# Attention unrolled, its small steps moved, and its transposing transfers cut in two

## The reference

```
qkv = (x @ Wqkv).reshape(b, l, 3, H, DH)          # 16 heads of 16 features
q = q * cos + rotate_half(q) * sin                # the same for k
scores = einsum("bqhd,bkhd->bhqk", q, k) * 16 ** -0.5
out = einsum("bhqk,bkhd->bqhd", softmax(scores), v).reshape(b, l, d) @ Wo
x = layernorm(x + out)
x = layernorm(x + ffn(x))      # a shared expert, and the top 2 of 8 experts per token
```

## Time and profile before

| | |
|---|---|
| median of 3 runs | 1282.6 us (1282.54 to 1285.19) |
| the profiled execution | 1286.31 us |
| its span, first to last instruction | 1284.4 us |
| mean granted TensorE clock | 0.969 |
| TensorE busy | 1174.9 us, 91% of the span |
| VectorE, ScalarE, GpSimd busy | 970.9, 895.0, 582.5 us |
| DMA | 194.45 MB, 260558 packets, 152256 of them under 512 B |
| transposing transfers (`att_qk<-att_stack`) | 128 |

### The profile page before, as it was taken

How to read it: one execution, slowest core, us unless ns; L and a number is a source line. 1 busy time by engine, 2 the same in 40 slices (tenths; PEclk the granted TensorE clock), 3 DMA queues, 4 the chain that set the end, 5 groups by cost and what they waited for, 6 DMA issues and landing times. The chain is left out here.

```text
span 1284.4 us, 27380 instructions
## 1 busy us (share of the span) xinstructions
PE 1174.9 (91%) x8369; PEld 864.1 (67%) x8416; DVE 970.9 (76%) x1868; ACT 895.0 (70%) x1970; POOL 582.5 (45%) x591
## 2 busy tenths in 40 slices
PE   3799898989898999879899969999999999999997
PEld 2333333333333333247899969999999999999897
DVE  4788787888787888738766658777777777777596
ACT  3377777777677777647744447777777777777686
POOL 5332222232223220006557745666666666666763
PEclk8699999999999999989899979999999999999999
DMA  6743525252537363532032256777777777776363
GB/s 151 137 82 58 112 53 97 63 110 61 130 96 159 85 155 88 170 125 85 17 112 92 96 170 220 258 237 235 249 251 252 237 238 234 249 252 207 131 187 114
DMA packets 260558, 194.45 MB, mean 151 GB/s; under 512 B 152256, under 2 KB 243392, under 8 KB 260480
## 3 DMA queue, kind: packets, MB, share of 16 engines
q1 hardware_dynamic: 253664, 174.82, 48.2%
q0 software_dynamic: 6816, 18.75, 4.1%
HBM read 122.06 MB, written 37.52 MB: 124 GB/s over the span
## 5 line engine op out<-in xcount | busy, mean ns | idle before, releaser
L464 ACT ACTIVATE att_prob<-att_psB 128x512 f32<-128x512 f32 x512 | 298.3, 608 | 133.1 <-PE att_psB L363 114.0
L553 DVE TENSOR_REDUCE att_mx<-att_psA 128x1 f32<-128x512 f32 x512 | 327.9, 681 | 77.3 <-PE att_psA L353 67.4
L353 PE MATMUL att_psA<-att_qk 96*128 96x512 bf16 x512 | 197.6, 390 | 17.6 <-DVE att_mx L553 6.9
L1650 ACT ACTIVATE exp_psU<-exp_psU,ew_b 128x256 f32<-128x256 f32 x312 | 126.9, 446 | 103.8 <-PE exp_psU L1607 103.8
L363 PE MATMUL att_psB<-att_qk 128*128 128x512 bf16 x465 | 178.4, 387 | 10.2 <-DMA att_qk<-att_mrow 6.1
L1701 DVE CAST exp_hh<-exp_psU 128x512 fp32r<-128x512 f32 x156 | 107.8, 691 | 102.4 <-ACT exp_psU L1650 102.4
L1590 PE MATMUL exp_psD<-exp_w2h,exp_hh 128*128 128x256 f32 x624 | 175.8, 282 | 0.0
L1605 PE MATMUL exp_psU<-exp_xh,exp_w1h 128*128 128x256 f32 x624 | 173.8, 279 | 1.4 <-DVE exp_xl L1692 1.4
L1606 PE MATMUL exp_psU<-exp_xl,exp_w1h 128*128 128x256 f32 x624 | 173.4, 278 | 0.0
L1607 PE MATMUL exp_psU<-exp_xh,exp_w1l 128*128 128x256 f32 x624 | 173.4, 278 | 0.0
L1591 PE MATMUL exp_psD<-exp_w2l,exp_hh 128*128 128x256 f32 x624 | 172.5, 276 | 0.0
(11 more groups left out here) (211 smaller groups left out, 2854.3 us busy)
## 6 DMA issues: line engine op xcount, KB each, us to landing
ew_w<-ew SPq DMA_DIRECT2D x40, 1024.0 KB, 4.9
exp_w<-ew SPq DMA_DIRECT2D x38, 1024.0 KB, 5.8
slots_x<-pre_acc SPq DMA_DIRECT2D x13, 780.0 KB, 4.4
pre_spare<-slots_x SPq DMA_DIRECT2D x39, 260.0 KB, 4.2
out_g<-rows_y SPq DMA_DIRECT2D x32, 256.0 KB, 3.9
ew_b<-eb SPq DMA_DIRECT2D x39, 128.0 KB
pre_spare<-xT SPq DMA_DIRECT2D x8, 512.0 KB, 3.9
attn_rows<-att_ob SPq DMA_DIRECT2D x8, 512.0 KB, 2.8
```

What stands on the lines that cost most here:

```text
L353: pe.matmul(psA[A_BANK[n % U]][:, :], r[:, 0, qt * P:(qt + 1) * P], r[:, 1, :], start=True, stop=True).then_inc(s_amm, 1)
L464: act.activation(prob[:, n % PR, :], psB[B_BANK[n % U]][:, :], ACT.Exp, scale=SCALE).then_inc(s_exp, 1)
L553: dve.reduce_max(mx[:, g % 2, n % U:n % U + 1], psA[A_BANK[n % U]][:, :], AX_X).then_inc(s_max, 1)
```

## The change

The loop goes: all periods are written out, and waits are on constants. A transposing transfer takes one group of four heads instead of eight heads, so there are eight to a tile. Tiles 2 and 3 get stacks of their own, in the buffer of the probabilities, and the first exponential waits until all four first tiles are turned. SyncE turns group 0 of these four tiles first, then group 1, and so on. In later sequences the parts of `qk` still being read are waited for group by group. Small steps move: x's high half from step 14 to step 0 of its period, and GpSimd's low half ahead of its sum; the copy of the maxima from 9 to 11; the output's turning from 5 to 6; the pieces one step earlier; the projection of Q and K from steps 0 and 1 to step 0 whole. The weights come in two transfers. The clearing of `slots_x`, the constants and the attention's rows are issued over many periods instead of at one place. The first step of `split_max` is another form of instruction. In the fill ScalarE makes pieces 1 and 2, which VectorE made before.

```diff
@@ numbers of the steps
-    PROJECT_QK, ROPE, COPY_OUT, TURN_OUT, NORM_OUT = (0, 1), (1, 1, 2), 3, 5, (5, 6)
-    PROJECT_V, COPY_V, SPLIT_MAX, TURN_MAX, COPY_MAX = 13, 13, 8, 10, 9
-    PIECE_1, SPREAD_1, PIECE_2, SPREAD_2, SPLIT_X = 7, (8, 9), 10, (11, 12), 14
+    PROJECT_QK, ROPE, COPY_OUT, TURN_OUT, NORM_OUT = 0, (1, 2, 2), 3, 6, (6, 7)
+    PROJECT_V, COPY_V, SPLIT_MAX, TURN_MAX, COPY_MAX = 13, 13, 8, 10, 11
+    PIECE_1, SPREAD_1, PIECE_2, SPREAD_2, SPLIT_X = 6, (7, 8), 9, (10, 11), 0
@@ the loop
-            for p in range(-QK_LEAD, HEAD):
-                period(p, None)
-            with eng.Fori(0, passes) as it:
-                for p in range(HEAD, HEAD + BODY):
-                    period(p, it)
...
+            for p in range(-QK_LEAD, NG + 1):
+                period(p)
@@ stacks of the first tiles
+        def stack_of(tile):
+
+            if tile in (2, 3):
+                some = prob[:, PR // 2 * (tile - 2):PR // 2 * (tile - 1), :].rearrange("p n l -> p (n l)").bitcast(BF16)
+                return some.rearrange("p (i h c) -> p i h c", i=2, h=H)
+            return stack[:, tile % 2]
@@ SyncE
-            def turn_heads(tile, half):
-
-                b, t, some = tile // NT, tile % NT, slice(half * HALF, half * HALF + HALF)
+            def turn_heads(tile, hg):
+
+                b, t, some = tile // NT, tile % NT, heads(hg)
...
+                    if b == 0:
+                        turn_heads(tile, 0)
+                        if t == NT - 1:
+                            for hg in range(1, HG):
+                                for first in range(NT):
+                                    turn_heads(first, hg)
+                    elif b > 1 and t == 0:
+                        for hg in (0, 1):
+                            turn_heads(tile, hg)
+                    elif b > 1 and t == 1:
+                        for hg in (0, 1):
+                            turn_heads(tile, hg)
+                        for hg in (2, 3):
+
+                            sp.wait_ge(s_bmm, U * (HG * (b - 2) + hg + 1))
+                            for late in (tile - 1, tile):
+                                turn_heads(late, hg)
+                    else:
+                        for hg in range(HG):
+                            turn_heads(tile, hg)
...
+                for b in range(B - 1):
+                    if p == max(NT * b + 6, ALL_CLEAR + b):
+                        sp.wait_ge(s_ost[b % 2], 16 * (b // 2 + 1))
+                        norm.load_attention(sp, attn_out, b)
                 if p == LOAD:
-                    sp.wait_ge(s_zero, 16 * CHUNKS)
                     sp.wait_ge(s_xl, B)
                     norm.load_constants(sp, x, Wo, norm_w, router_wT)
...
@@ GpSimd
+                if t == NT - 1 and valid(b + 1 - 2, B - 2):
+                    x_lo(b + 1)
                 if tile >= FILL:
-                    wait(pool, it, s_qrd, tile + 1, 1)
+                    wait(pool, s_qrd, tile + 1)
                     pool.tensor_tensor(rr[:, :], rc[:, :], rs[:, :], ALU.add).then_inc(s_rr, 1)
...
-                if t == NT - 1 and valid(tile + 1 - 2 * NT, NT * (B - 2)):
-                    x_lo(b + 1, it)
@@ ScalarE
+                if n == 0:
+                    for hg in range(HG):
+                        for k in range(2):
+                            act.wait_ge(s_tr[hg][k], 32 * NT // 2)
...
+            def piece_1(tile):
+                wait(act, s_rr, tile + 1)
+                if tile >= FILL:
+                    for hg in range(HG):
+
+                        wait(act, s_tr[hg][tile % 2], 32 * (tile // 2))
...
@@ VectorE
-                    link(dve.tensor_scalar(mstk[:, 0, :], m, -1.0, None, ALU.mult))
+                    link(dve.scalar_tensor_tensor(mstk[:, 0, :], m, 0.0, m, ALU.mult, ALU.subtract))
```

More of the change, by code:

```diff
@@ L131, in attention, with aside @@
         psX = a.ps("psX", [P, 512], F32)
-        s_w = a.sem("w_loaded")
+        ASIDE_QK, ASIDE_V = {1: psA[0], 2: psB[0], 3: psB[1]}, {0: psA[1], 1: psA[2]}
+        def aside(tile, value):
+            return (ASIDE_V if value else ASIDE_QK).get(tile)
+        s_w = [a.sem(f"w_loaded{i}") for i in range(2)]
         s_tab = a.sem("tables_loaded")
@@ L149, in attention @@
         s_ost = [a.sem(f"o_stored{i}") for i in range(2)]
-        s_tr = [[a.sem(f"heads_turned{half}{k}") for k in range(2)] for half in range(2)]
+        s_tr = [[a.sem(f"heads_turned{hg}{k}") for k in range(2)] for hg in range(HG)]
         s_msp = a.sem("max_split")
@@ L166, in attention, with wait, groups @@
         s_dve = a.sem("vector_chain")
[L168 to L178, removed]
-            for p in range(-QK_LEAD, HEAD):
-                period(p, None)
-            with eng.Fori(0, passes) as it:
-                for p in range(HEAD, HEAD + BODY):
-                    period(p, it)
[L185 to L188, removed]
+        def wait(eng, s, v):
+            if v > 0:
+                eng.wait_ge(s, v)
+        def groups(period):
+            for p in range(-QK_LEAD, NG + 1):
+                period(p)
         def valid(i, n):
@@ L313, in x_lo, with put @@
-            def x_lo(b, it):
-                v = b + 1
-                pool.wait_ge(s_xh, v if it is None else v + it * 2)
+            done = [0]
+            def put(ins):
+                ins.then_inc(s_init, 1)
+                done[0] += 1
+                pool.wait_ge(s_init, done[0])
+            for tile in range(NT):
+                put(pool.memset(stack_of(tile)[:, :, :, KR:], 0.0))
+                put(pool.memset(stack_of(tile)[:, 1, :, KR:KR + PIECES], 1.0))
+            assert done[0] == PADDED
@@ new lines, in _ @@
+            put(pool.memset(zero, 0.0))
+            assert done[0] == BLANK
+            for one in (ident, identf):
+                put(pool.memset(one[:, :], 0.0))
+                put(pool.affine_select(out=one[:, :], in_=one[:, :], compare_op=ALU.not_equal, fill=1.0,
+                                       base=0, pattern=[[-1, P]], channel_multiplier=1))
+            put(pool.memset(V[:, :, :, :, DH + 1:], 0.0))
+            put(pool.memset(V[:, :, :, :, DH:DH + 1], 1.0))
+            put(pool.memset(norm.eps[:, 0:1], 1e-5))
@@ L436, in period @@
-            def period(p, it):
+                if tile == 0:
+                    pe.wait_ge(s_xh, 1)
+                    pe.wait_ge(s_wh, 2 if value else 1)
+                for c in range(DC):
+                    pe.matmul(o, xh[:, b % 2, c, rows], wh[:, c, cols], start=(c == 0), stop=False)
+                if tile == 0:
+                    pe.wait_ge(s_wl, 2 if value else 1)
+                for c in range(DC):
+                    pe.matmul(o, xh[:, b % 2, c, rows], wl[:, c, cols], start=False, stop=False)
@@ L437, in period @@
+                if t == 0 and not value:
+                    pe.wait_ge(s_xl, b + 1)
+                for c in range(DC):
+                    m = pe.matmul(o, xl[:, b % 2, c, rows], wh[:, c, cols], start=False, stop=(c == DC - 1))
+                m.then_inc(s_vmm if value else s_qmm, 1)
+            def period(p):
                 for u in range(U):
@@ L514, in period @@
+            w_hi(1, slice(2 * D, 3 * D))
+            x_hi(1)
+            def period(p):
                 for u in range(U):
```

358 lines of the change are left out of this document (150 added, 208 removed).

## The result

| | before | after |
|---|---|---|
| median of 4 runs each, on the same chip | 1283.9 us | 1340.1 us |
| range of the runs | 1282.54 to 1286.56 | 1338.08 to 1341.73 |
| span of the profiled execution | 1284.4 us | 1337.1 us |
| mean granted clock | 0.969 | 0.948 |
| first and last exponential | 58.9, 560.1 | 79.3, 615.2 |

The ratio is 1.0434, with a 95% interval of 1.0408 to 1.0461: slower by 4.3%. The forecast was 1268 us in a range of 1253 to 1288, so both the sign and the range were wrong. Two of the three signs that the prediction set for being wrong are there: the issue stays above 0.95 us, and ScalarE's first copy waits over 2 us for a transfer in every fourth period. The last exponential comes 55.1 us later and the span is 52.7 longer, so the loss is all in the attention.

What follows compares the result with a forecast made beforehand. TensorE was taken to set the pace, VectorE and ScalarE close behind. Gains of 27.4 us less 7.0 (fill), 4 (late group) and 2.5 (last periods) made -13.9 us: forecast 1268 us, range 1253 to 1288.

Steps and rivals of the forecast that it cites:

- the three signs: Forecast wrong if transposing issue stays above 0.95 us, ScalarE's first copy waits over 2 us every fourth period, or plain period exceeds 15.6.
- the price c: SyncE's time from one half-size transposing transfer's issue to the next: taken as 0.78 us, bounds 0.69 and 1.38.
- the formula of the fill: Before the first exponential: X, when the transfer that tile 4's first copy awaits lands; 45.9 us at 0.78 an issue.
- X + 20.0: Time of the first exponential, 20.0 us after that transfer lands: 65.9 us, a loss of 7.0.
- the late group: Twelve transfers in one period of four, six times; ScalarE's first copy of tile 2 waits 0.9 us; 4 us charged in all.
- Rival one: Fill and late group: a half-size transposing instruction costs nearly the same; 1321 us at 1.38 an issue; chance 0.12.
- (1): TensorE's waits for the low half of x, 11.0 us in six, go; with the branch stall, 22.2 us gained.
- (2): ScalarE's 3.64 us idle after the loop's branch, twice, goes; with the x stall, 22.2 us gained.
- the last group's wait: TensorE's 5.22 us wait at 548.02, behind seven loads issued ahead of the last placing, goes: gain 5.2 us.
- The plain period: An attention period without stalls, 15.27 us: edits cancel, taken as unchanged, bounds -0.3 and +0.4 us.
- The cost of the later copy: In the plain period: V projection waits some 0.45 us for the copy of the maxima; placings end 0.2 us late.
- Periods 26 to 29: The last four, shorter periods: the later placing is last to arrive, +0.6 us each, 2.5 in all.

Runs made afterwards that it cites:

- experiment 3: The kernel before, with trial transposing transfers of several sizes issued by SyncE ahead of everything; issue 1.21 to 1.23 us from one head to eight, 1.88 at sixteen.
- the eight-head version: The kernel after with eight heads to a transposing transfer again (128 in all, turned by halves), every other edit kept: 1267.1 us, ratio 0.9847.

## Why the prediction was wrong

**The step that failed is the price c.** The prediction bounded it by 0.69 and 1.38 and took 0.78, "nearer to the low end because the copy's issue time belongs to the whole instruction and a transposing one is more than twice as long, which its size must cause". Nothing showed that last clause. The transposing transfer is slower to issue than a copy, and its size is not the reason: experiment 3 has 1.21 us at an eighth of it. The other argument, that 16 transfers moved data without a break, was no evidence for size either: at eight heads the issue (1.29) and the data of one transfer happen to take nearly the same time, so that both look like the bound. c was 1.31.
The Trainium skill ("DMA: Bandwidth & Descriptors", "Why a DMA increments its semaphore by 16 and not by 1") has one push per tile for a transpose in the earlier generations. That row is for 8,192 tiles. By that rule a price follows the number of tiles, and at the sizes here the traces disagree: 1.217 us for half the tiles against 1.287, and 1.214 for an eighth (experiment 3). The rule in the same page's "Rules for kernel authors", to coalesce, points the right way; its 64 KB is not where it ends here, since these transfers went from 256 to 128 KB and saved 0.07 us each.

**The mechanisms around c were right.** With c = 1.31 the formula of the fill, X = 28.0 + 23c, gives 58.1, and 58.93 was measured; X + 20.0 to the first exponential was 20.4. For the late group 14.3 + 10c + 1.4 - 22.6 gives 6.2, and 6.9 was measured; the places, the six times and the queue behind ScalarE's copy were as described. Rival one was therefore the true story, with a chance of 0.12 that came from the wrong reading of c.

**Rival one was still 19 us short** (1321 against 1340). Periods 0 to 24 hold this: they take 442.8 us, about 20 more than its terms give.
- 9 are in the late group. Rival one charged it with its waits, 6 x 6.9 = 41; the six periods stand at 142.9 where six plain ones of 15.46 would be 92.8, so 50. Some 5 of the 9 are there without any such wait: in the eight-head version the six take 97.6, because x's high half now stands ahead of the next period's first exponential. This leaves 4 for the clock behind each wait.
- 6 are in the other 19 periods, in periods 6 and 7 above all: with 256 transfers they take 18.1 and 17.3 us, with 128 15.4 and 15.7. In period 6 eight transposing transfers take 11.73 us of SyncE, and the next load of x is issued 1.2 us ahead of the placing (7.5 in the eight-head version). The placing then lands 4.5 us after its issue, where it takes 1.7 in a plain period, and TensorE waits 2.46 us for it. In the eight-head version the longest such wait in these two periods is 0.5.
- 5 are the plain period, 0.19 longer in each of 25.

**The gains came.** (1) and (2) were 22.2 us together; alone they give 1.26 and 0.31% of 1285, 20 us. Of the last group's wait of 5.2, 4.6 went, and its period is 5.2 shorter.

**The plain period** was forecast as unchanged, within -0.3 and +0.4, and is +0.19. That is right as a sum, but in part by luck. The cost of the later copy was well sized: 0.45 for the V projection and 0.2 for the placings, and 0.6 was measured for both together. So was the gain: 0.5 for the split and the output together, and 0.5 came back when their columns were put back; only the new form of the instruction had no part in it. But one term was missing: the projection in one block costs 0.3, and the prediction had nothing for it. The measured parts, +0.6, +0.3 and -0.5, add up to +0.4; what made it 0.2 less was not separated. Above all, the parts were written down as cancelling and not as two edits, of which one could be left out. Periods 26 to 29 take 3.0 us more, where 2.5 were forecast, with the copy as the cause: with it at 9 they take 52.7 us instead of 56.0.

## What to carry to other kernels

Before a transfer is cut, find out whether its issue price has a size in it; if one size is all that the trace has, then both ends stay equally likely, and the queue behind it must be priced with the full one. Count queue positions, not bytes: what a waiter pays is the position of the transfer it needs, times the issue, and every reordering moves that position. An edit whose parts cancel on paper is two experiments; here one number of a schedule was worth 1 to 2% in each of three kernels.

## What the runs showed of the hardware

- A transposing DMA issued by SyncE holds it 1.2 to 1.25 us at the median for 1 to 8 blocks of 128 x 128 (2 bytes an element), and 1.20 and 1.18 for 8 blocks of 64 and of 32 rows. In experiment 3 the second of two with sixteen heads took 3.55 us. In the full kernels single issues are longer at the smaller sizes too: 11 of the 256 in the kernel after took 1.8 to 2.6 us.
- Its landing is 2.4 us for one or two heads and 4.4 for sixteen.
- Removing a stall of 3.6 us behind a loop's branch was worth 2.2 and 2.9 us over the pair of periods around it, and 5 us were lost again in three other periods, in which the granted clock behind a wait of 2.0 us was 0.76 instead of 1.00.
- Three placings of 4 KB each landed 4.2 to 4.9 us after their issue close behind a load of x and a clearing transfer, and 1.7 after it in a plain period.
- VectorE's first step of the split (128x16) took 0.96 us as TENSOR_SCALAR and 1.05 as SCALAR_TENSOR_TENSOR beside GpSimd's subtraction, and 0.164 away from it.
- Behind 9 us in which TensorE was busy for 4.22, the granted clock was 0.70 over the next 7 us; behind the five other waits of this kind it was 0.50 to 0.60.
